# Two pre-norm graph layers on one Trainium2 core: x kept on chip for the residual sum in place of an accumulating store

## What is computed

```python
h = jnp.maximum(_layernorm(x, axis=-1), 0.0)
x = x + L0(h, adj, adj, b)                  # one number per node, see below
h = jnp.maximum(_layernorm(x, axis=-1), 0.0)
x = x + L1(h, w_qkv, w_proj, b_proj, gamma, beta, adj)
```

```python
ln = (o - mu) * rsqrt(var + LN_EPS) * gamma + beta
return o + ln
```

## Time and profile before

| | us |
|---|---|
| median of 3 runs | 779.43 |
| lowest and highest run | 777.5 and 783.04 |
| the profiled execution, its own time | 781.43 |
| its span | 779.7 |
| PE busy in the span | 724.6 |
| DVE busy | 606.4 |
| ACT busy | 466.1 |
| POOL busy | 395.3 |

### The profile page before, as it was taken

How to read it: one execution, slowest core, us unless ns; L and a number is a source line. 1 busy time by engine, 2 the same in 40 slices (tenths; PEclk the granted TensorE clock), 3 DMA queues, 4 the chain that set the end, 5 groups by cost and what they waited for, 6 DMA issues and landing times.

```text
span 779.7 us, 37319 instructions
## 1 busy us (share of the span) xinstructions
PE 724.6 (93%) x16233; PEld 490.2 (63%) x16233; DVE 606.4 (78%) x1458; ACT 466.1 (60%) x1033; POOL 395.3 (51%) x720
## 2 busy tenths in 40 slices
PE   1789999999999999999999999999999999999851
PEld 0356666666666666666666666666666766666540
DVE  3568888787888888888888888888888888878642
ACT  4456675556666655667666556676665566774420
POOL 4324455554556455554564554545545546454433
PEclk9999999999999999999999999999999999999975
DMA  6333335535544665464455544543455345424222
GB/s 191 104 84 84 59 83 110 111 87 108 70 86 96 112 110 96 99 112 77 77 98 110 111 93 102 111 70 81 102 111 111 87 108 110 84 38 77 29 28 28
DMA packets 102835, 71.01 MB, mean 91 GB/s; under 512 B 68369, under 2 KB 101905, under 8 KB 102161
## 3 DMA queue, kind: packets, MB, share of 16 engines
q1 hardware_dynamic: 85776, 51.85, 26.9%
q0 software_dynamic: 16896, 16.78, 16.7%
HBM read 35.06 MB, written 33.55 MB: 88 GB/s over the span
## 4 chain that ended last, share of the span: by engine, by line
PE 90%; DVE 3%; ACT 2%; issue 2%; DMA 1%; POOL 1%; SPq 0%; DVEq 0%; POOLq 0%
PE a_ps L309 21%; PE sum_ps L427 11%; PE a_ps L321 11%; PE pv_ps L396 8%; PE sum_ps L399 7%; PE sc_ps L375 6%; PE sc_ps L350 6%; PE sc_ps L330 6%; PE a_ps L291 5%; PE sum_ps L424 3%; PE pv_ps L411 2%; PE sc_ps L379 2%; PE sc_ps L356 1%; DVE smax L649 1%; DMA w_sb<-in_L_gnn_w_qkv 1%
## 5 line engine op out<-in xcount | busy, mean ns | idle before, releaser
L542 ACT ACTIVATE p_sb<-sc_ps 128x512 f32<-128x512 f32 x256 | 140.4, 607 | 37.2 <-PE sc_ps L379 37.2
L649 DVE TENSOR_REDUCE smax<-sc_ps 128x4 f32<-128x512 f32 x256 | 157.6, 677 | 1.8 <-PE sc_ps L350 1.8
L834 POOL TENSOR_TENSOR oT_lo<-oT,oT_hi 128x256 f16<-128x256 f32 x128 | 83.4, 672 | 132.1 <-ACT oT_hi L555 132.1
L309 PE MATMUL a_ps<-hT,w_hi 128*128 128x512 f16 x512 | 133.2, 383 | 5.9 <-DMA hT<-h_parts 3.2
L548 ACT ACTIVATE pv_sb<-pv_ps 128x512 f32<-128x512 f32 x64 | 38.2, 597 | 144.6 <-PE sum_ps L399 144.6
L637 DVE TENSOR_TENSOR qk_lo<-a_ps,qk_hi 128x512 f16<-128x512 f32 x128 | 87.4, 683 | 29.7 <-ACT qk_hi L529 29.5
L396 PE MATMUL pv_ps<-p_sb,v_sb 128*32 128x128 f32 x2048 | 104.9, 276 | 1.9 <-ACT pv_sb L548 1.3
L399 PE MATMUL sum_ps<-p_sb,sel_sum 128*32 128x128 f32 x2048 | 103.4, 273 | 0.0
L687 DVE BATCH_NORM_STATS2 st<-o_sb 128x6 f32<-128x256 f32 x128 | 53.6, 420 | 49.5 <-ACT o_sb L561 49.4
L828 POOL TENSOR_TENSOR h_parts<-h_sb,h_parts 128x256 f16<-128x256 f32 x128 | 82.1, 673 | 18.8 <-ACT h_parts L507 18.7
L529 ACT ACTIVATE qk_hi<-a_ps 128x512 f16<-128x512 f32 x128 | 77.4, 604 | 9.4 <-PE a_ps L309 9.3
(11 more groups left out here) (106 smaller groups left out, 1772.7 us busy)
## 6 DMA issues: line engine op xcount, KB each, us to landing
x_sb<-in_x SPq DMA_DIRECT2D x32, 512.0 KB, 5.4
out<-in_x SPq DMA_DIRECT2D x32, 512.0 KB, 5.5
out<-y_sb POOLq DMA_DIRECT2D x32, 512.0 KB, 6.2
w_sb<-in_L_gnn_w_qkv SPq DMA_DIRECT2D x1, 768.0 KB, 6.7
hT<-h_parts SPq DMA_TRANSPOSE x33, 4.6
wp_sb<-in_L_gnn_w_proj SPq DMA_DIRECT2D x1, 256.0 KB, 5.4
gamma_sb<-in_L_gnn_ln_gamma SPq DMA_DIRECT2D x1, 128.0 KB, 5.9
beta_sb<-in_L_gnn_ln_beta SPq DMA_DIRECT2D x1, 128.0 KB, 6.8
```

The costliest lines, as they stand in the source:

```text
L309: mm = nc.tensor.matmul(a_ps[c % 2][:].rearrange("p (b n) -> p b n", b=G), w[:, dc, col:col + P], hT[:, par, part, :, dc], start=(k == 0), ...
L542: nc.scalar.activation(p_sb[:, j, i], sc_ps[i][:], ACT.Exp, scale=SCALE).then_inc(p_ready, 1)
L649: nc.vector.tensor_reduce(smax[:, i, 0, j], sc_ps[i][:], AX.X, ALU.max).then_inc(smax_ready, 1)
L834: nc.gpsimd.tensor_tensor(oT_lo[:, b], oT[:, b], oT_hi[:, b], ALU.subtract).then_inc(olo_ready, 1)
```

## The change

The copy of x into the output and its semaphore go, and the output's DMA no longer accumulates. `x_sb` has six slots in place of three, and x stays there until DVE's last addition, which now reads it in the place of beta. POOL adds beta to x in its slot, one group a step (four instructions of 128x256 f32), at the end of its step; DVE's first y_sb of a group waits for the four. The output goes out by plain DMAs from SP, in two halves of a group of 256 KB each, behind the second and the fourth y_sb. SP's order is `X0 T0 D0 D1`; the load of group t+3 waits for the y_sb of the group that had its slot.

```diff
--- before.py
+++ after.py
 SLOTS = 3
+X_SLOTS = 6
...
-        x_sb = sb("x_sb", [P, SLOTS, G, D])
+        x_sb = sb("x_sb", [P, X_SLOTS, G, D])
...
         @block.sync
-            def copy_x(t):
-                wait(sp, copied, 16 * t)
-                nc.sync.dma_start(out.rearrange("(g b) n d -> g (b n) d", b=G)[t],
-                                  x.rearrange("(g b) n d -> g (b n) d", b=G)[t]).then_inc(copied, 16)
-            def load_x(t, par):
-                wait(sp, h_ready, G * (t - 2))
+            def load_x(t):
+                wait(sp, y_ready, G * (t - X_SLOTS + 1))
                 sp.wait_ge(x_loaded, 16 * t)
-                nc.sync.dma_start(x_sb[:, par], xg[t]).then_inc(x_loaded, 16)
+                nc.sync.dma_start(x_sb[:, t % X_SLOTS], xg[t]).then_inc(x_loaded, 16)
+
+            def store(g, i):
+                sp.wait_ge(y_ready, G * g + 2 * (i + 1))
+                half = slice(2 * i, 2 * i + 2)
+                nc.sync.dma_start(og[g][:, half], y_sb[:, half]).then_inc(stored, 16)
...
-            ORDER = ("C0 T0 X0").split()
+            ORDER = ("X0 T0 D0 D1").split()
...
-                    if kind == "C" and a:
-                        copy_x(t)
+                    if kind == "D" and d:
+                        store(t - 2, i)
                     elif kind == "T" and prep:
                         transpose_h(t + 1, (k + 1) % SLOTS)
                     elif kind == "X" and load:
-                        load_x(t + 3, k)
+                        load_x(t + 3)
...
             pipeline(step)
+            sp.wait_ge(stored, 32 * STEPS)
...
         @block.vector
                         if b == 0:
-                            wait(dve, stored, 16 * g)
-                        nc.vector.scalar_tensor_tensor(y_sb[:, b], t_sb[:, b], base2[:, b:b + 1], beta_sb[:],
-                                                       ALU.add, ALU.add).then_inc(y_ready, 1)
+                            wait(dve, stored, 32 * g)
+                            dve.wait_ge(xb_ready, G * (g + 1))
+                        nc.vector.scalar_tensor_tensor(y_sb[:, b], t_sb[:, b], base2[:, b:b + 1],
+                                                       x_sb[:, g % X_SLOTS, b], ALU.add, ALU.add).then_inc(y_ready, 1)
...
         @block.gpsimd
-            def store(g):
-                pool.wait_ge(copied, 16 * (g + 1))
-                pool.wait_ge(y_ready, G * (g + 1))
-                nc.gpsimd.dma_start(og[g], y_sb[:], accum_op=ALU.add).then_inc(stored, 16)
+            def add_beta(g, b):
+                if b == 0:
+                    pool.wait_ge(h_ready, G * (g + 1))
+                nc.gpsimd.tensor_tensor(x_sb[:, g % X_SLOTS, b], x_sb[:, g % X_SLOTS, b], beta_sb[:], ALU.add).then_inc(
+                    xb_ready, 1)
...
-            ORDER = ("C0 C1 C2 C3 H0 H1 H2 H3 N0 W0 W1 W2 K0 W3 D0 X0").split()
+            ORDER = ("C0 C1 C2 C3 H0 H1 H2 H3 N0 W0 W1 W2 K0 W3 X0 B0 B1 B2 B3").split()
...
-                    elif kind == "D" and d:
-                        store(t - 2)
+                    elif kind == "B" and e:
+                        add_beta(t - 1, i)
...
             pipeline(step)
-            pool.wait_ge(stored, 16 * STEPS)
```

More of the change, by code:

```diff
@@ L198, in build @@
         tw_ready = sem("tw_ready")
-        copied = sem("copied")
+        xb_ready = sem("xb_ready")
         y_ready = sem("y_ready")
@@ L269, in step @@
                     elif kind == "X" and load:
-                        load_x(t + 3, k)
-            load_x(1, 1)
+                        load_x(t + 3)
+            load_x(1)
             first_transposes()
-            load_x(2, 2)
+            load_x(2)
             pipeline(step)
+            sp.wait_ge(stored, 32 * STEPS)
         @block.tensor
@@ L498, in rectify @@
                     wait(act, hlo_ready, G * t)
-                nc.scalar.activation(h_sb[:, b], x_sb[:, par, b], ACT.Relu, bias=shift1[:, par, b:b + 1],
+                nc.scalar.activation(h_sb[:, b], x_sb[:, t % X_SLOTS, b], ACT.Relu, bias=shift1[:, par, b:b + 1],
                                      scale=rstd1[:, par, b:b + 1]).then_inc(h_ready, 1)
@@ L612, in _, with stats_x @@
             nc.vector.memset(mhalf[:], -0.5).then_inc(dve_const, 1)
-            def stats_x(t, par):
+            def stats_x(t):
                 dve.wait_ge(x_loaded, 16 * (t + 1))
@@ L617, in stats_x @@
                 for b in range(G):
-                    nc.vector.bn_stats(st1[:, b], x_sb[:, par, b]).then_inc(stats1, 1)
+                    nc.vector.bn_stats(st1[:, b], x_sb[:, t % X_SLOTS, b]).then_inc(stats1, 1)
             def aggregate_x(t):
@@ L744, in step @@
                         if i == 0:
-                            stats_x(t + 2, (k + 2) % SLOTS)
+                            stats_x(t + 2)
                         else:
@@ L790, in later_constants @@
                     nc.vector.tensor_copy(bp_rows[HD * i:HD * i + 1], bp_parts[HD * i:HD * i + 1, i]).then_inc(dve_const, 1)
-            stats_x(0, 0)
+            stats_x(0)
             aggregate_x(0)
@@ L795, in _ @@
             mask_constants()
-            stats_x(1, 1)
+            stats_x(1)
             aggregate_x(1)
```

## The result

| | before | after |
|---|---|---|
| median of the runs (range) | 779.85 us (777.5 to 783.04), 4 runs | 795.15 us (793.19 to 795.32), 4 runs |
| profiled execution, own time | 781.43 us | 795.28 us |
| its span | 779.7 us | 793.3 us |
| one ordinary step | 22.32 us | 22.85 us |
| last y_sb to the end of the span | 7.7 us | 2.6 us |

The change makes the kernel slower by 1.85%: the ratio after to before is 1.0185, with a 95% interval from 1.0154 to 1.0215. The forecast was 777.5 us.

What follows compares the result with a forecast made beforehand. TensorE (PE), busy 93% of the span, was taken as the bound. From the median 779.43 us, -1.3 (end -3.4, last steps +2.1) and -0.6 for gaps gave 777.5 us; own range 773.6 to 781.0, 8 in 10 773 to 789.

Steps and rivals of the forecast that it cites:

- What runs beside the additions: Ordinary step: POOL's additions delay DVE's cast and rpair 0.2 us each, under 0.46 slack; 0 per step, at most 0.9.
- the sum: Whole kernel: -3.4 + 2.1 = -1.3 us, 0.6 more off the median 779.43; 777.5 us, range 773.6 to 781.0.
- rival (a): Body: additions collide with cast and rpair, PE loses 0.35 us in some 29 steps; 787.5 us, chance 0.33.
- Traffic, the middle of the kernel: Body: removed copies and accumulation were hidden, SP's new loads and stores delay nothing; counted at nothing for PE.
- POOL in an ordinary step: Four additions of 0.67 us from 421.3 to 424.0 us, 1.1 us before o_low; cost 0, bounds 0 and 0.1.
- The last three steps: From step 30, additions meet DVE's t_sb and y_sb at 0.3 us each; tail loses 2.1 us, bounds 0 and 3.3.
- The end: Behind DVE's last addition: SP's 256 KB store makes 7.7 us into 4.35, a gain of 3.4 (bounds 1.7 and 3.8).
- The gaps called issue: Early steps: PE gaps no instruction releases, 4.0 us excess; 0.6 us taken off, bounds 0 and 2.0.
- (b): Copies and accumulation cause PE's gaps; all excess vanishes, tail gains in full without meetings; 773.6 us, chance 0.12.
- (c): Nothing moves: the last store takes 5.4 us like a body load, DVE's last steps lose 2.1; 779.8 us, chance 0.15.

Runs made afterwards that it cites:

- run 1: Kernel after, with POOL's four additions moved from behind invert_std_x to the idle gap between h_low and normalise_o; 774.76 us, ratio to before 0.9934.
- 6: Kernel after, with additions 0 and 1 left behind invert_std_x and 2 and 3 moved between h_low and normalise_o; 776.9 us.
- 7: Kernel after, with additions 0, 1 and 2 left behind invert_std_x and only 3 moved between h_low and normalise_o; 792.35 us.
- run 3: Kernel after, with four POOL memsets of a scratch buffer in place of the additions, beta left out; 774.99 us.
- run 10: Kernel before, copy and accumulation kept, plus four POOL additions into scratch behind invert_std_x; 799.69 us, beside 782.23.
- 5: Kernel after, with POOL's additions waiting for the rpair that DVE does in that same stretch; 781.02 us.
- run 9: Kernel of run 1, with one 512 KB store a group issued from POOL ahead of invert_std_x; 780.82 us, beside 782.23 for the kernel before.
- run 2: Kernel after without the additions, beta missing from the output, DVE's last addition waiting for h_sb; 773.59 us, ratio to before 0.9924.
- run 8: Kernel of run 1, with one 512 KB store a group from SP in place of two halves; 776.07 us, ratio to before 0.9936.

## Why the prediction was wrong

**The step that failed is "What runs beside the additions".** It charged the cast and rpair 0.2 us each, 0.4 in all, under a slack of 0.46 us, and so a cost of 0 per step. Measured (runs after, 1, 6 and 7): the cast pays 0.34 us and rpair 0.57, together 0.91 us. The cover is a little less than the 0.46 us that the prediction took, because L413 begins 0.06 us after rpair ends even when it waits for nothing else: 0.40 us. So 0.51 us are left, and the step is 0.53 us longer. 28 steps of it are 14.8 us, close to the 15.3 us between the medians only because the other parts of the change nearly cancel.

The 0.22 us came from t_sb beside w_sb. It was taken as what a meeting costs, while it is what that meeting cost, with that partner: w_sb has one tensor input, an addition has two. Whether this is what makes the difference no run shows. The upper bound of the step, 2 x 0.67 - 0.46 = 0.9 us, held the result, though the sum's own range (773.6 to 781.0 us) left it out: 0.9 us in 28 steps is 25 us more, and the phases in the earlier trace rows were enough to place it: the cast falls into the first addition, and rpair onto the start of the third. That arithmetic stood in the prediction, as rival (a), and came out but for its sizes. It had rpair end near 423.7 us, 1.0 us late; in the like phase the delay was 0.91. It then took 0.35 us as PE's loss, though 1.0 - 0.46 is 0.54. That this is nearly the measured 0.53 is in part luck, as its delay is 0.09 us too long and its cover 0.06 too large. So rival (a)'s 787.5 us was too low by its own numbers: with 0.53 us in 29 steps it would have been 792.9.

The Trainium skill, SBUF — State Buffer, section "Who interferes with whom", says that where a DVE instruction with two inputs in SBUF meets a GpSimd one that reads SBUF, or DVE is in a 2-port mode, the second to issue blocks fully. The runs agree in kind: in the kernel after both of DVE's instructions end with an addition (406.07 and 407.50 us beside 405.98 and 407.38), and in run 3 the cast, by the page a 2-port operation, is blocked by memsets that only write. The cast came second in both, which fits what the page says of issue order. They do not bear out the whole of it: in the last steps of the kernel after an instruction of DVE and an addition take 0.87 us together and not 1.09, and in run 3 and in the last steps of run 10 DVE is held up by the whole train of four and not by the first.

**Traffic, the middle of the kernel**: right. With the additions in the gap the step is 22.32 us with the new loads and stores, in halves or whole, from SP or POOL.

**POOL in an ordinary step**: right. An addition took 0.71 to 0.73 us for 0.67, the four began at 405.25 us (421.33 on the clock of the prediction, which said 421.3), and 1.33 us were left before o_low (1.1 forecast). Runs 5 and 10 show what happens when this cover goes: 0.20 and 0.33 us a step.

**The last three steps**: the same mis-sized term. 0.3 us per meeting was 0.46, so four meetings cost 1.85 us and not 1.2. With the covers of 1.10, 0.38 and 0 us that is 0.75, 1.5 and 1.85, 4.1 in all, and 4.24 were measured, against 2.1 forecast and 3.3 as the bound. To it come 0.85 us at the end, where the clock is slower, which nobody could read from the rows.

**The end**: right in kind, too small in size. The term 0.1 + 3.7 + 0.55 = 4.35 us was 2.6 us: the store lands 2.3 us after its issue, not 3.7. The gain was 5.1 us, not 3.4. The 0.1 us from the addition to the issue held for SP, though not "wherever these rows show one": POOL's DMA in the earlier trace rows began 0.97 us after its addition. A load, and even the 64 KB load of adj (3.3 us), was no lower bound for a store. By the Trainium skill, DMA: Bandwidth & Descriptors, section "Anatomy of one DMA — SWDGE (gpsimd) path", the estimate was 2.6 us to landing; the measured 2.3 is near that, and for 512 KB from SP the same formula gives 3.2 us (an estimate) against 3.7 measured. The page gives the formula for DMAs issued by gpsimd, and there it is further off: 3.2 us against 5.1 in run 9.

**The gaps called issue**: the change took none for certain. In one profile each, the 28 steps behind the fourth transposes take 4.1 us more than 28 x 22.32 before, 1.4 in run 1, 1.3 in run 2, 1.8 in run 8 and 3.7 in run 9; after, there is about nothing over 28 x 22.85. What sets them stays open; it was not tried by itself.

**Rivals (b) and (c)** fall with the body: both had it untouched. Without the collision the parts of the change come out as in run 1: 774.76 us, 2.7 us under the forecast. The end accounts for 5.1 - 3.4 = 1.7 us of this, and 2.1 us were forecast for meetings in the last steps that run 1 does not have; against them its profile has 1.7 us more in the last two stretches, where PE's clock stays at 0.50 longer than before.

## What to carry to other kernels

Where work is added to POOL, lay its instructions beside DVE's in time and look at every overlap with a two-input or cast instruction of DVE. In this kernel a meeting with one addition of 0.71 us cost 0.34 to 0.57 us, somewhat less than what was left of the addition; but twice, in runs 3 and 10, one instruction was held up by a whole train of four, for up to 3 us. So take the rest of the one POOL instruction as the middle of the estimate and the rest of the train as its bound; a shorter lengthening beside another instruction is no price. Compare the sum with the slack of whoever waits for DVE, and if it does not fit, look for a stretch in which DVE reads PSUM or one operand: the same four additions cost 0.53 us a step in one place and nothing in another. When a rival's arithmetic and its price disagree, work the price out again before giving it a chance.

## What the runs showed that was not expected

- Which instruction is met matters more than how many: with two additions at the old place the step is 22.32 us, with three 22.87, and the fourth changes nothing (22.85).
- A memset on POOL, which reads nothing, holds DVE's cast for 0.67 us (0.90 for 0.23), over all four memsets, where the additions of the kernel after held it only to the end of the first (0.58). In the last three steps of run 10 additions too held a cast or rpair over all four (2.50, 3.16 and 3.30 us).
- A plain store of 256 KB from SP lands in 2.3 us, one of 512 KB in 3.7; from POOL 512 KB land in 5.1.
- PE's granted clock in two short stretches differs between kernels whose instructions there are the same. Between 37 and 42 us it was 1.00 in seven of the twelve kernels' profiles and 0.66 to 0.71 in five (before the one, after the other, the faster run 1 also the other). The distance from the second to the third transposes goes with it without exception: 17.28 to 17.29 us in the seven, 18.76 to 18.85 in the five:

```profile
37.00:42.00 5.00, 4.95 (x89) 2.24 (x90) 0.69 (x1) 1.89 (x5) 0.00 (x0) 0.66 0.02 3
```

```profile
37.00:42.00 5.00, 5.00 (x98) 2.42 (x95) 1.04 (x2) 3.44 (x8) 0.00 (x0) 1.00 0.08 32
```

The first is the kernel after, the second the one before. In what the engine did ahead of it (32 to 37 us) the two are alike, 2.78 and 2.73 us busy, and what tips it stays open.
